# A decoder layer on one core: the head groups of the last 16 tiles turned by transposing DMAs, rows ordered by batch through a permuting product

## What is computed

```python
# layer 0: weights quantized to a codebook of 64 values, plus a low-rank part
lora_delta = lora_B @ lora_A * 0.5
normalized = (weight + lora_delta).reshape(512, 4, 128) / exp(scale_log)
idx = searchsorted(thresholds, normalized); w_eff = cb[idx] * scale + lora_delta
x = x + x @ w_eff.T
# layer 1: attention over a paged cache of 512 keys and 32 new ones, 32 query heads, 8 key heads, D = 128
q, k, v = x @ Wq.T, x @ Wk.T, x @ Wv.T
q, k = rope(rmsnorm(q, q_norm_w), pos), rope(rmsnorm(k, k_norm_w), pos)
kc, vc = k_cache[block_table], v_cache[block_table]          # 16 pages of 32 a batch
scores = q @ concat([kc, k]).T * D ** -0.5, cached keys masked behind cache_seqlens
o = softmax(scores) @ concat([vc, v])
x = x + o @ Wo.T
```

## Time and profile before

| what | us |
|---|---|
| timed runs, median of 3 | 2192.24 |
| timed runs, lowest and highest | 2188.72, 2193.31 |
| profiled execution | 2179.66 |
| its span | 2177.6 |
| PE busy in the span | 2108.1 |
| DVE, ACT, POOL busy | 1717.1, 1478.2, 1281.7 |

### The profile page before, as it was taken

The page is one execution under the profiler, slowest core; times in us unless marked ns, Lnnn a source line. Parts: engine busy times, 40 slices in busy tenths (PEclk is TensorE's granted clock), DMA queues, the critical chain, the costliest instruction groups (busy, mean ns, idle before and its releaser), DMA issues.

```text
span 2177.6 us, 60484 instructions
## 1 busy us (share of the span) xinstructions
PE 2108.1 (97%) x17634; PEld 1371.4 (63%) x17634; DVE 1717.1 (79%) x3902; ACT 1478.2 (68%) x4966; POOL 1281.7 (59%) x2101
## 2 busy tenths in 40 slices
PE   6979889999999999999998999999999999999998
PEld 2435466666666666666665666666666666666665
DVE  8986588888888788888876777778777777777785
ACT  4834477777777777777775766666777766666664
POOL 7002156766666666666765666666666666666663
PEclk9989999999999999999999999999999999999999
DMA  8988587789988998988898687666666676676663
GB/s 231 333 270 265 168 209 208 216 225 233 235 219 227 205 235 228 228 216 233 215 277 219 180 263 189 185 191 186 180 187 177 180 199 187 177 195 183 182 186 103
DMA packets 553804, 458.70 MB, mean 211 GB/s; under 512 B 127861, under 2 KB 482500, under 8 KB 552710
## 3 DMA queue, kind: packets, MB, share of 16 engines
q1 hardware_dynamic: 433062, 295.67, 48.6%
q0 software_dynamic: 40960, 134.25, 20.4%
q10 hardware_dynamic: 79456, 24.91, 7.3%
HBM read 377.21 MB, written 56.70 MB: 199 GB/s over the span
## 4 chain that ended last, share of the span: by engine, by line
PE 83%; DMA 1%; SPq 1%; DVE 1%; issue 1%; ACT 0%; POOL 0%; DVEq 0%; ACTq 0%
PE PR L1330 21%; PE Op L1311 15%; PE WOp L1363 15%; PE Sp L1277 15%; PE PTp L1288 11%; PE TRp L1340 2%; PE Sp L1280 1%; PE Op L1293 1%; PE Op L1313 1%; SPq L755 1%; DMA wsrc<-in_L_cond_Wo 0%; DMA wsrc<-in_L_cond_Wq 0%; PE WOp L1348 0%; DMA weights_split<-wsrc 0%; DVE masked L1530 0%
## 5 line engine op out<-in xcount | busy, mean ns | idle before, releaser
L736 POOL DMA_INDIRECT pages<-values_split,rows x512 | 522.2, 1020 | 123.4 <-issue 114.9
L1330 PE MATMUL PR<-Wt,xT 128*128 128x512 f16 x2232 | 539.1, 380 | 0.1
L1414 ACT ACTIVATE pts<-PTp 128x512 f16<-128x512 f32 x512 | 305.8, 597 | 326.2 <-PE PTp L1288 324.8
L1311 PEld LDWEIGHTS Op<-pts,pages 128*128 128x128 f16 x6144 | 385.6, 98 | 128.4 <-DVE OT L1548 7.6
L1311 PE MATMUL Op<-pts,pages 128*128 128x128 f16 x6144 | 427.3, 219 | 8.7 <-DVE OT L1548 5.1
L1277 PE MATMUL Sp<-pages,qT 128*128 128x512 f16 x1536 | 417.1, 380 | 6.9 <-PEq L183 6.9
L1535 DVE TENSOR_TENSOR pts<-PTp,pts 128x512 f16<-128x512 f32 x512 | 351.6, 687 | 75.2 <-ACT pts L1414 74.7
L1530 DVE CUSTOM_DVE_ANT_0 masked<-Sp,mask 128x544 f32<-128x544 f32 x512 | 370.2, 723 | 51.0 <-PE Sp L1280 41.2
L1420 ACT ACTIVATE masked<-masked,small 128x544 f32<-128x544 f32 x512 | 379.3, 741 | 19.9 <-DVE small L1530 19.2
L1363 PE MATMUL WOp<-WoT,OT 128*128 128x512 f16 x1536 | 377.5, 379 | 0.0
L1330 PEld LDWEIGHTS PR<-Wt,xT 128*128 128x128 f16 x2232 | 218.5, 98 | 187.9 <-issue 1.7
(11 more groups left out here) (252 smaller groups left out, 2962.4 us busy)
## 6 DMA issues: line engine op xcount, KB each, us to landing
pages<-keys_transposed SPq DMA_DIRECT2D x2048, 64.0 KB
mask<-mask_rows SPq DMA_DIRECT2D x128, 128.0 KB
v<-new_values SPq DMA_DIRECT2D x96, 128.0 KB
...
pages<-values_split,rows POOLq DMA_INDIRECT x512
```

What stands on the lines that cost most here:

```text
L736: nc.gpsimd.indirect_dma_start(out=vS[:, n % 2, c, :, :].rearrange("p l n -> p (l n)"), out_offset=None, in_=v_d, in_offset=bass.IndirectO ...
L1311: nc.tensor.matmul(o, vS[:, par, c, low, h * D:(h + 1) * D], pts[:, u % 2, part, c * P:(c + 1) * P], start=(k == 0), stop=False)
L1330: m = nc.tensor.matmul(bank(k), xT[:, c, xl, :], Wp[:, c, wl, GROUP_COL[k]:GROUP_COL[k] + HID], start=(i == 0), stop=(i == NPASS - 1))
L1414: nc.scalar.activation(pts[:, u % 2, 0, :], PTp[:, :], ACT.Copy).then_inc(G.pt_hi, 1)
```

## The change

**In the tiles.** From prepared tile 15 on (`all_by_dma`; 16 tiles of 31) no group is turned by PE. ACT copies the high part of `qr` into the left half of a 128x1024 buffer (`split_high`), DVE subtracts the low part into its right half (`queries_low`), and a transposing DMA from ACT's queue writes the whole group to `qT` (`turn_by_dma`). The buffers are `split` for the keys and for the last group, `wdst` and the two halves of `wsrc` for the others. The issues stand at the ends of slots 12 to 15 and of slot 0 of the next tile. PE waits for head group h at the first score that reads it (`heads_turned`).

**Rows by batch.** The rows within a tile now stand in the order position, batch: `turn_x1` multiplies by a permutation `by_position` in the place of the identity, the rope positions pass through the same permutation, and the new values are stored and loaded in that order. `qT` becomes `[2, KVH, 2, REP * P]`, and the scores of all tiles read every fourth column (`b::BPT`) of the queries and of the new keys. The copies out of `TRp` in the first half's tiles write side by side.

**In the setup.** ACT and DVE copy the doubled rows (ACT's for phase 1 between the masks), eight angle steps stand between the masks, the jumps are made ready ahead of `norm`, the third chunk of the caches is loaded without a wait, and a bank's scale and last sum are four operations of 128 columns.

Cut to its core:

```diff
-    squares={1: 0, 3: 1, 6: 3, 8: 4, 10: 5}, values=5, values_low=6, keys_low=6,
+    squares={1: 0, 3: 1, 6: 3, 8: 4, 10: 5}, values=5, values_low=6, split={6: 0, 7: 1, 10: 3, 12: 4, 14: 5}, keys_low=6, queries_low={7: 1, 11: 3, 13: 4, 15: 5}, issue={12: 0, 13: 1, 14: 3, 15: 4, 16: 5},
...
-        qT = sb("qT", [P, 2, 2, KVH * REP * P], F16)
+        qT = sb("qT", [P, 2, KVH, 2, REP * P], F16)
...
+        by_position = scr[:, 1088:1216]
+        pos_rows = scr[:, 3376:3392]
...
+                pe.wait_ge(G.const_done, 5)
+                pe.wait_ge(G.positions, 4)
+                nc.tensor.matmul(PR[:, 1, 0:TILES], by_position, pos, start=True, stop=True).then_inc(G.positions_ordered, 1)
+                pe.wait_ge(G.positions_taken, 1)
...
-                a.wait_ge(G.norm_done_first, 1)
-                for phase in range(2):
-                    rows_of = norm[64 * phase:64 * phase + 64, :]
-                    for half in range(2):
-                        a.dma_start(pair_rows[phase][64 * half:64 * half + 64, :], rows_of).then_inc(rows_paired[phase], 16)
+                for i in range(2):
+                    cols = slice(i * 2 * HID, (i + 1) * 2 * HID)
+                    a.wait_ge(G.norm_done_first, i + 1)
...
+                    if 8 <= step < 24 and step % 4 == 2:
+                        half, i = divmod((step - 8) // 4, 2)
+                        cols = slice(i * 2 * HID, (i + 1) * 2 * HID)
+                        nc.scalar.activation(pair_rows[1][64 * half:64 * half + 64, cols], norm[64:128, cols], ACT.Copy).then_inc(G.rows_paired_1, 1)
...
+                    V.tensor_copy(pair_rows[0][64:128, cols], norm[0:64, cols]).then_inc(G.rows_paired_0, 1)
...
-                for step in range(6):
-                    angles(step)
+                v.wait_ge(G.positions_ordered, 1)
+                V.tensor_copy(pos_rows, PR[:, 1, 0:TILES]).then_inc(G.positions_taken, 1)
...
-                    if step in (1, 3):
-                        angles(6 + step // 2)
+                    if step % 2 == 0 and step < 16:
+                        angles(step // 2)
...
-                    V.tensor_tensor(a_.rearrange("p (g i) -> p g i", i=P), a_.rearrange("p (g i) -> p g i", i=P),
-                                    scale_t[:, 4 * k:4 * k + 4].rearrange("p (g o) -> p g o", o=1).to_broadcast([P, 4, P]), ALU.mult).then_inc(G.weff_chain, 1)
-                    v.wait_ge(G.weff_chain, 3 * k + 3)
-                    V.tensor_tensor(a_, a_, delta[:, c0:c1], ALU.add).then_inc(G.weff_done, 1)
+                    v.wait_ge(G.weff_chain, 2 * k + 2)
+                    for g_ in range(4 * k, 4 * k + 4):
+                        group = slice(g_ * P, (g_ + 1) * P)
+                        m = V.scalar_tensor_tensor(acc[:, group], acc[:, group], scale_t[:, g_:g_ + 1], delta[:, group], ALU.mult, ALU.add)
+                    m.then_inc(G.weff_done, 1)
...
+                m = by_position.rearrange("p (n b) -> p n b", b=BPT)
+                Q.affine_select(out=m, in_=m, compare_op=ALU.not_equal, fill=1.0, base=0, pattern=[[-1, S], [-S, BPT]], channel_multiplier=1).then_inc(G.const_done, 1)
...
-                sp.dma_start(v5[place * S:(place + 1) * S, tile % 2, :, :], vn_d[tile % 2, part].rearrange("(b p) n -> p b n", b=BPT)).then_inc(v5_loaded[tile % 2], 16)
+                sp.dma_start(v5[place * S:(place + 1) * S, tile % 2, :, :], vn_d[tile % 2, part].rearrange("(p b) n -> p b n", b=BPT)).then_inc(v5_loaded[tile % 2], 16)
...
-                            m = nc.tensor.transpose(Sp[:, c * P:(c + 1) * P], x1b[t % 2][:, c * P:(c + 1) * P], ident[:, :])
+                            m = nc.tensor.matmul(Sp[:, c * P:(c + 1) * P], x1b[t % 2][:, c * P:(c + 1) * P], by_position, start=(c == 0), stop=(c == IC - 1))
...
+            def all_by_dma(ti):
+                return ti >= TILES - 1
+
+            def low_done(ti, k):
+                far = ti - (TILES - 1)
+                return (G.split_low, ti + 1) if k == 0 else (G.queries_low, far * QUERY_GROUPS + NORMED.index(k))
+
+            def split_no(ti, k):
+                far = ti - (TILES - 1)
+                return TILES - 1 + far * len(NORMED) + NORMED.index(k) if far >= 0 else ti
+
+            def split_buffer(k):
+                if k in (0, 5):
+                    return split[:, :, :].rearrange("p l n -> p (l n)")
+                return wdst[:, :, :].rearrange("p l n -> p (l n)") if k == 1 else wsrc[:, (k == 4) * 1, :].bitcast(F16)
+
+            def turned_heads(nt, k):
+                if k == 0:
+                    return kTn[:, nt, :, :].rearrange("p l (h n) -> p (l h) n", h=KVH)
+                return qT[:, nt, NORMED.index(k) - 1, :, :].rearrange("p l (r n) -> p (l r) n", r=REP)
+
             with nc.Block() as block:
...
-                            pe.wait_ge(G.tr_lo, QUERY_GROUPS * (u // UPT))
+                            pe.wait_ge(G.tr_lo, QUERY_GROUPS * min(u // UPT, TILES - 1))
                             pe.wait_ge(G.keys_turned, 16 * (u // UPT))
-                        q0 = (h * BPT + b) * P
+                        if b == 0 and u // UPT >= TILES:
+                            pe.wait_ge(heads_turned[h], 16 * (u // UPT - TILES + 1))
+                        q = [qT[:, tt, h, part, b::BPT] for part in range(2)]
                         for k, (ql, kl) in enumerate(((0, 0), (0, 1), (1, 0))):
-                            nc.tensor.matmul(Sp[:, 512:1024].rearrange("p (a n) -> p a n", a=NPP), qT[:, tt, ql, q0:q0 + P], kT[n % KBUFS][:, :, h, kl, :],
+                            nc.tensor.matmul(Sp[:, 512:1024].rearrange("p (a n) -> p a n", a=NPP), q[ql], kT[n % KBUFS][:, :, h, kl, :],
                                              start=(k == 0), stop=(k == 2))
                         for k, (ql, kl) in enumerate(((0, 0), (0, 1), (1, 0))):
-                            m = nc.tensor.matmul(Sp[:, 512 - S:512], qT[:, tt, ql, q0:q0 + P], kTn[:, tt, kl, h * P + b * S:h * P + (b + 1) * S], start=(k == 0), stop=(k == 2))
+                            m = nc.tensor.matmul(Sp[:, 512 - S:512], q[ql], kTn[:, tt, kl, h * P + b:(h + 1) * P:BPT], start=(k == 0), stop=(k == 2))
                         m.then_inc(G.qk_done, 1)
...
-                        if ti in proj and sl in plan["turn"]:
+                        if ti in proj and sl in plan["turn"] and not all_by_dma(ti):
...
+                    def split_high(ti, k):
+                        far = ti - (TILES - 1)
+                        a.wait_ge(G.rope_done, norm_no(ti, k) + 1)
+                        if k == 0:
+                            if ti >= 1:
+                                a.wait_ge(G.keys_turned, 16 * ti)
+                            if far >= 1:
+                                a.wait_ge(heads_turned[3], 16 * far)
+                        elif k == 5:
+                            a.wait_ge(G.keys_turned, 16 * (ti + 1))
+                        elif far == 0:
+                            a.wait_ge(G.w_moved, 16 * PIECES)
+                            a.wait_ge(G.w_stored, 16 * PIECES)
+                        else:
+                            a.wait_ge(heads_turned[NORMED.index(k) - 1], 16 * far)
+                        nc.scalar.activation(split_buffer(k)[:, 0:HID], qr[:, norm_no(ti, k) % 2, :], ACT.Copy).then_inc(G.split_high, 1)
+
+                    def turn_by_dma(ti, k):
+                        a.wait_ge(*low_done(ti, k))
+                        done = G.keys_turned if k == 0 else heads_turned[NORMED.index(k) - 1]
...
-                        if ti in proj and sl in plan["turned"]:
-                            rotated_high(ti, tt, plan["turned"][sl])
+                        if ti in proj and all_by_dma(ti) and sl in plan["split"]:
+                            split_high(ti, plan["split"][sl])
+                        elif ti in proj and not all_by_dma(ti) and sl in plan["turned"]:
+                            if plan["turned"][sl] == 0:
+                                split_high(ti, 0)
+                            else:
+                                rotated_high(ti, tt, plan["turned"][sl])
...
-                            if sl == plan["keys"]:
-                                a.wait_ge(G.split_low, ti + 1)
-                                a.dma_start(kTn[:, 1 - tt, :, :].rearrange("p l (h n) -> p (l h) n", h=KVH), split[:, :, :].rearrange("p l n -> p (l n)"), transpose=True).then_inc(G.keys_turned, 16)
+                            if sl in plan["issue"] and (sl == plan["keys"] or all_by_dma(ti)):
+                                turn_by_dma(ti, plan["issue"][sl])
+                        if sl == 0 and ti - 1 in proj and all_by_dma(ti - 1):
+                            turn_by_dma(ti - 1, plan["issue"][UPT])
...
+                    def queries_low(ti, k):
+                        v.wait_ge(G.split_high, split_no(ti, k) + 1)
+                        halves = split_buffer(k)
```

(1 more changed line is left out.)

63 lines of the change are left out of this document (32 added, 31 removed).

## The result

The changed kernel takes **2280.8 us** in the median of six runs (2265.6 to 2296.7) where the kernel before, in the same series, takes 2191.6: a ratio of **1.041** (95% interval 1.036 to 1.046). Forecast was 2173. The profiled execution took 2276.3 us (span 2274.5). The profiled execution of the kernel before (2179.66 us) lies 12 us under its median, so differences against its trace come out somewhat too large.

A forecast was written before the change was run, and what follows sets the result against it. PE was taken to bound the tiles, PE and DVE the stretches before. Terms -28.2 + 3 + 0 + 9 - 3 = -19.2 us took the 2192.2 us median to 2173 us; range 2158 to 2210.

The forecast's parts named there:

- Transposes off PE: Last 16 prepared tiles: four groups each lose a set of four PE transposes, 0.44 us a set, -28.2 us.
- ACT's issues: Four new DMA issues a tile on ACT's queue, covered by its 18 us free a tile: 0; uncovered 32 us.
- Late landings: Waits on transposing DMAs: one or two stalls about tile 16, tenths elsewhere, +3 us; ends 0 and +28.
- (a): ACT's slot 14 copy waits about 0.7 us for the keys' transpose, issued in slot 12, to finish reading its buffer.
- (b): PE waits for head group 0 at the next tile's first score, 8.6 us after issue; groups 1 to 3 similar.
- Rival B: Transposes land late: at 9.8 us each tile stalls 1.2 us, 19 us in all, 2192, no change; chance 0.11.
- Strided reads: All 512 units read queries and new keys at a step of four f16 elements: 0, +64 us kept for the range.
- rival A: Strided loads are slow, 32-column products wait for weights: +43 to +64 us, 2216 to 2237; chance 0.17.
- First block: Transposes of x1 become f32 products with a permutation, +0.6 us in each of 16 steps: +9 us, ends 0 and +17.
- Setup: Before the first block: row copies, angle steps, less DMA traffic and split bank operations together -3 us, ends -8 and +3.
- -1.3 for 2 MB less: Before the first block, DMA engines at 1.00 move 2 MB less: -1.3 us within the setup's sum.

The follow-up runs named there:

- gathers first: Early issues plus late copy of group 5, with POOL issuing slot 11's gathers before group 4's rotation sum and ACT copying group 4 after the exponential: 2179.6 us.
- early issues: Changed kernel with only issue slots moved in the last 16 tiles: groups in slots 7, 11, 13 and 15, keys in 9: 2204.8 us, ratio 1.0047.
- idle ones: Kernel with PE's turns in all tiles, plus four unread transposing DMAs a tile in the last 16, issued in slots 7, 11, 13 and 15: 2218.3 us.

## Why the prediction was wrong

Along one chain of runs, each taken against the kernel before in its own series: rows by batch and setup +7.7; leaving PE's transposes -20.1 (from +7.7 to -12.4 with gathers first); the gathers' late landing, with the order of ACT's copies, +21.3 (to +8.9 with early issues); crowded and late transposes +80.3. That these come to +89.2, the measured loss, holds by their making; in another order of edits the parts could differ.

1. **Transposes off PE, -28.2: right in size.** Tiles fall from 59.63 to 57.87, 16 x 1.76 = 28 us, wherever nothing else is late. The changed kernel comes near it in one tile (58.00). Of the 28 us 20.1 arrive in the time of the run with gathers first, in whose trace PE still waits 6.3 us in these tiles.
2. **ACT's issues, 0: wrong.** The step took the one issue of before (1.25 us) for each of five in a row. While others are under way an issue lasts up to 14.5 us; 17 of the 64 for groups lasted over 2 us. Spread out, the longest of 64 idle ones took 2.26.
3. **Late landings, +3 with an end at +28: the step that failed.** The mechanism was named rightly: (a) and (b) are both in the trace, and the lead was as worked out (8.6 us; in the changed kernel 8.4 to 9.1 in the median of each group, from its issue to the moment when PE is ready for it). Mis-sized was the landing. It was read from the keys' transpose, one a tile in these tiles before: median 6.7 us; with five in a row it was 9.4, up to 23.4, in the group that the profile tells of. The upper end was "the gain is gone", which bounds nothing: a late group costs its whole wait, and what stands behind it on ACT comes later too, as in tile 22. Tiles 15 to 30 took 1023.4 us, where 16 x 57.87 would be 926. Of the 97 us more, 74.3 are waits of PE, and some 20 are an estimate of what the lower clock costs there (0.98 of 1023 us, 1.00 before). And a third wait was missed: the traffic also delays another queue's transfers, the gathers that slot 15 reads, 18.2 us in the changed kernel. Nothing in the trace of before waited for them, so they had no row. Rival B, which the prediction gave a chance of 0.11, named the cause and priced 1.2 us a tile; PE's waits came to 4.6 (74.3 / 16).
4. **Strided reads, 0: wrong by a little.** 0.29 us a tile, 18 ns a unit, 32 x 0.29 = 9 us in the traces, and 8.9 in the times for the whole row order; half of the 37 ns from which rival A decides. The Trainium skill ("Advanced Engine Details and Errata", SBUF Cachelines) promises full speed from two accesses in a 16-byte line; at a step of 8 bytes the load took 113 ns and not 98, so here the measurement decides.
5. **First block, +9: right in the trace, not in the time.** 0.45 us a step (0.89 - 0.44), and a first score product 4.9 us later than with the old row order (266.8 against 261.9); but a permutation as transpose gave back only 0.8 us of time, as tile 0 became longer by what the block gave back. The advice of the Trainium skill ("Perfetto Trace Analysis", Transposes) to make logical transposes PE transposes holds for a permutation too, in that block's own time.
6. **Setup, -3: not seen.** The first block starts 1.5 us earlier (156.56 against 158.08), but with the old row order (156.96) the first score product still came 3.2 us later than in the trace of before, and the time is the same (0.9998). One term, -1.3 for 2 MB less, follows from no row: at the 343 GB/s of the earlier trace rows 2 MB are some 6 us.

The range ended at 2210 since every case but A treated a landing as an addend of a few microseconds.
